# Row maxima of the attention scores, turned by VectorE in 32 by 32 blocks in place of TensorE

## The reference

```python
scores = jnp.einsum('bhqd,bhkd->bhqk', Q, K) / scale
scores = jnp.where(mask, scores, NEG_INF)
attention = jax.nn.softmax(scores, axis=-1)
heads_out = jnp.einsum('bhqk,bhkd->bhqd', attention, V)
```

## Time and profile before

| | |
|---|---|
| runs | 1285.56, 1286.76 (median) and 1288.77 us |
| span of the profiled execution | 1284.1 us, 2.7 us under the median of the runs |
| busy in it | PE 94%, DVE 70%, ACT 55%, POOL 37% of the span |
| TensorE's granted clock, mean | 0.987 |
| transfers `QS<-NT` | 64, of 12 KB each |

### The profile page before, as it was taken

One profiled execution on the slowest core, in us unless ns is written; L12 is line 12 of the kernel. 1 busy time (PEld: TensorE's weight loads), 2 busy tenths in 40 slices (PEclk: granted clock), 3 DMA queues, 4 the chain that ended last, 5 costly groups with the idle time before them and its releaser, 6 DMA issues.

```text
span 1284.1 us, 25175 instructions
## 1 busy us (share of the span) xinstructions
PE 1213.3 (94%) x9260; PEld 859.1 (67%) x9260; DVE 893.2 (70%) x2680; ACT 710.7 (55%) x1197; POOL 481.3 (37%) x675
## 2 busy tenths in 40 slices
PE   7899999999999989999999989999999999988998
PEld 6577666666767654444458866677676776578987
DVE  4677677876787646589999856767867868652333
ACT  2455555555655538889973426666566566622221
POOL 5534333443443100067000334344643643322555
PEclk9899999999999999999999999999999999998999
DMA  6423333233432041000004653355455342137973
GB/s 194 127 77 105 91 93 108 88 105 98 123 88 67 11 128 55 1 1 2 1 1 130 177 157 108 108 152 147 129 167 136 113 134 72 51 145 241 311 194 39
DMA packets 121942, 137.22 MB, mean 107 GB/s; under 512 B 12882, under 2 KB 116428, under 8 KB 121798
## 3 DMA queue, kind: packets, MB, share of 16 engines
q1 hardware_dynamic: 111888, 125.98, 33.2%
q0 software_dynamic: 7296, 8.15, 3.5%
q10 hardware_dynamic: 2634, 1.49, 0.5%
HBM read 58.42 MB, written 27.36 MB: 67 GB/s over the span
## 4 chain that ended last, share of the span: by engine, by line
PE 55%; DVE 6%; issue 3%; ACT 2%; POOL 1%; SPq 1%; DMA 1%; ACTq 0%; POOLq 0%; DVEq 0%
PE PS L669 14%; PE PS L715 6%; PE PS L470 5%; PE PS L410 5%; PE PS L683 4%; PE PS L453 4%; PE PS L429 4%; PE PS L528 2%; PE PS L724 2%; PE PS L502 2%; PE PS L417 2%; DVE NM L1119 1%; PE PS L546 1%; ACT P L839 1%; PE PS L511 1%
## 5 line engine op out<-in xcount | busy, mean ns | idle before, releaser
L839 ACT ACTIVATE P<-PS 128x512 f32<-128x512 f32 x512 | 302.4, 601 | 165.8 <-PE PS L456 100.2
L1116 DVE CUSTOM_DVE_ANT_0 MX<-PS,NQ 128x256 bf16<-128x256 f32 x512 | 192.5, 418 | 73.3 <-PE PS L429 73.0
L453 PE MATMUL PS<-QS,KS 99*128 99x256 bf16 x1024 | 226.6, 275 | 7.7 <-ACT P L839 6.7
L1119 DVE TENSOR_REDUCE NM<-PS 128x2 f32<-128x512 f32 x256 | 173.5, 685 | 74.6 <-PE PS L429 72.9
L429 PE MATMUL PS<-KS,QS 96*128 96x256 bf16 x1024 | 196.9, 275 | 21.6 <-DVE NM L1116 13.4
L429 PEld LDWEIGHTS PS<-KS,QS 96*128 96x128 bf16 x1024 | 87.2, 98 | 86.6 <-DVE NM L1116 26.1
L470 PE MATMUL PS<-P,V 128*32 128x256 f32 x2048 | 137.7, 387 | 1.5 <-ACT P L839 1.5
L453 PEld LDWEIGHTS PS<-QS,KS 99*128 99x128 bf16 x1024 | 95.4, 99 | 53.3 <-ACT P L839 20.1
L456 PE MATMUL PS<-NK,identb 128*128 128x256 bf16 x512 | 128.2, 275 | 0.0
L669 PE MATMUL PS<-XNT,wup 128*128 128x512 f16 x576 | 124.9, 379 | 0.0
L669 PEld LDWEIGHTS PS<-XNT,wup 128*128 128x128 f16 x576 | 56.2, 98 | 67.3
(11 more groups left out here) (233 smaller groups left out, 2473.6 us busy)
## 6 DMA issues: line engine op xcount, KB each, us to landing
KS<-PP SPq DMA_DIRECT2D x192, 128.0 KB, 2.9
QS<-PP SPq DMA_DIRECT2D x192, 128.0 KB, 2.5
WH<-in_wex SPq DMA_DIRECT2D x16, 768.0 KB, 8.0
WG<-in_wex SPq DMA_DIRECT2D x10, 768.0 KB, 5.1
bufd<-bias_row SPq DMA_DIRECT2D x5, 1032.0 KB, 12.0
XB<-in_x SPq DMA_DIRECT2D x16, 256.0 KB, 2.8
CT<-in_ctxT SPq DMA_DIRECT2D x16, 256.0 KB, 3.1
x1d<-XB SPq DMA_DIRECT2D x16, 256.0 KB, 2.1
```

Source lines behind the costliest of these rows:

```text
L453: ins = tensor.matmul(o, t.KS[b % 3][0:99, h, 128 * kt:128 * kt + 128], t.QS[b % 3][0:99, h, :], start=True, stop=(L == 1))
L839: scalar.activation(t.P[h % 8][:, :, :], PS[:, h % 2, :].rearrange("p (k n) -> p k n", k=2), ACT.Exp).then_inc(s_ex, 1)
L1116: ins = vector.tensor_tensor_reduce(t.MX[:, 2 * (h % 2) + qt, :], PS[:, bk, 256 * qt:256 * qt + 256], t.NQ[b % 4][:, qt, :], -1.0, 1.0e30, ...
L1119: ins = vector.tensor_reduce(nm[:, :, h], PS[:, bk, :].rearrange("p (t n) -> p t n", t=2), X, ALU.max, negate=True)
```

## The change

TensorE no longer turns the maxima, and ACT no longer copies them. The parts stand in `NP` as 32 columns for each of the two query tiles (24 used, 8 zeroed once for each layer by `pool_pad`). A new function `dve_maxima` transposes `NP`, 128 by 64, into `NT` with one DVE instruction, which turns each 32 by 32 block by itself. `NT` then has in its partition block `i` (32 partitions, 24 of them used) the queries 32i to 32i+31 of both tiles. So `act_maxima` issues four transfers in place of one, a block each, and each piece that lies together in memory on the `QS` side is 32 numbers, 64 bytes, in place of 256 numbers, 512 bytes. `pe_scores_t` waits for 64 counts in place of 16. Everything else stands as it was.

```diff
-            t.NT = [tile(m, f"NT{i}", [24, 256], BF16) for i in range(2)]
+            t.NT = [tile(m, f"NT{i}", [128, 64], BF16) for i in range(2)]
...
-            t.NP = tile(m, "NP", [128, 2, 3, 8], BF16)
+            t.NP = tile(m, "NP", [128, 2, 32], BF16)
...
-        def pe_maxima(L, b, hh):
-            n, t = L * NB + b, TL[L]
-            bk = odd_bank(("nt", n, hh), s_nt, 2 * n + hh + 1)
-            pe.wait_ge(s_np, 2 * n + hh + 1)
-            for qt in range(2):
-                ins = tensor.transpose(PSH[0:24, bk, 128 * qt:128 * qt + 128],
-                                       t.NP[:, qt, :, :].rearrange("p a h -> p (a h)"), identb[:, :])
-            ins.then_inc(s_ntr, 1)
...
-            pe.wait_ge(d_n[h // 8][b % 3], 16 * uses(L, b, 3))
+            pe.wait_ge(d_n[h // 8][b % 3], 64 * uses(L, b, 3))
...
-            for b, hh in maxima_at(L, s, k, 10, 2):
-                pe_maxima(L, b, hh)
...
         def act_maxima(L, b, hh):
             n, t = L * NB + b, TL[L]
-            bk = home["nt", n, hh]
-            if b:
-                act.wait_ge(d_n[hh][(b - 1) % 3], 16 * uses(L, b - 1, 3))
-            act.wait_ge(s_ntr, 2 * n + hh + 1)
-            scalar.activation(t.NT[hh][:, :], PSH[0:24, bk, 0:256], ACT.Copy).then_inc(s_nt, 1)
-
             act.wait_ge(s_nt, 2 * n + hh + 1)
             act.wait_ge(s_st, 16 * (n - 2))
-            scalar.dma_start(t.QS[b % 3][96:99, 8 * hh:8 * hh + 8, :], t.NT[hh][:, :]).then_inc(d_n[hh][b % 3], 16)
+            dst = t.QS[b % 3][96:99, 8 * hh:8 * hh + 8, :].rearrange("a h (t i r) -> a h t i r", t=2, i=4)
+            for i in range(4):
+                scalar.dma_start(dst[:, :, :, i, :], t.NT[hh][32 * i:32 * i + 24, :].rearrange("p (t r) -> p t r", t=2)).then_inc(
+                    d_n[hh][b % 3], 16)
...
+        def dve_maxima(L, b, hh):
+
+            n, t = L * NB + b, TL[L]
+            if b:
+                dve.wait_ge(d_n[hh][(b - 1) % 3], 64 * uses(L, b - 1, 3))
+            dve.wait_ge(s_pad, L + 1)
+            dve.wait_ge(s_np, 2 * n + hh + 1)
+            vector.transpose(t.NT[hh][:, :], t.NP[:, :, :].rearrange("p t c -> p (t c)")).then_inc(s_nt, 1)
...
             for h in scores_at(L, s, k):
                 dve_max(L, s + 1, h)
+            for b, hh in maxima_at(L, s, k, 10, 2):
+                dve_maxima(L, b, hh)
```

More of the change, by code:

```diff
@@ L339, in build @@
         d_n = [[sem(f"d_n{i}{j}") for j in range(3)] for i in range(2)]
-        d_i, s_iv = sem("d_i"), sem("s_iv")
+        d_i, s_iv, s_pad = sem("d_i"), sem("s_iv"), sem("s_pad")
         s_av, s_pen, s_var, s_rs, s_xn, s_xb = (sem(n) for n in ("s_av", "s_pen", "s_var", "s_rs", "s_xn", "s_xb"))
@@ L343, in build @@
         s_hi, s_r1, s_mid, s_lo = (sem(n) for n in ("s_hi", "s_r1", "s_mid", "s_lo"))
-        s_s, s_mx, s_np, s_ntr, s_nt = (sem(n) for n in ("s_s", "s_mx", "s_np", "s_ntr", "s_nt"))
+        s_s, s_mx, s_np, s_nt = (sem(n) for n in ("s_s", "s_mx", "s_np", "s_nt"))
         s_st, s_ex, s_ah, s_ot = (sem(n) for n in ("s_st", "s_ex", "s_ah", "s_ot"))
@@ L1649, in pool_maxima, with pool_pad @@
             v = t.NM[b % 2][:, :, 8 * hh:8 * hh + 8]
+            parts = [t.NP[:, :, 8 * a:8 * a + 8] for a in range(3)]
             pool.wait_ge(s_mx, 16 * n + 8 * hh + 8)
-            pool.wait_ge(s_ntr, i)
-            gpsimd.tensor_copy(t.NP[:, :, 0, :], v).then_inc(*pool.tick())
+            pool.wait_ge(s_nt, i)
+            gpsimd.tensor_copy(parts[0], v).then_inc(*pool.tick())
             pool.wait_ge(*pool.last())
-            gpsimd.tensor_tensor(t.NR[:, :, :], v, t.NP[:, :, 0, :], ALU.subtract).then_inc(*pool.tick())
+            gpsimd.tensor_tensor(t.NR[:, :, :], v, parts[0], ALU.subtract).then_inc(*pool.tick())
             pool.wait_ge(*pool.last())
-            gpsimd.tensor_copy(t.NP[:, :, 1, :], t.NR[:, :, :]).then_inc(*pool.tick())
+            gpsimd.tensor_copy(parts[1], t.NR[:, :, :]).then_inc(*pool.tick())
             pool.wait_ge(*pool.last())
-            gpsimd.tensor_tensor(t.NP[:, :, 2, :], t.NR[:, :, :], t.NP[:, :, 1, :], ALU.subtract).then_inc(s_np, 1)
+            gpsimd.tensor_tensor(parts[2], t.NR[:, :, :], parts[1], ALU.subtract).then_inc(s_np, 1)
+        def pool_pad(L):
+            gpsimd.memset(TL[L].NP[:, :, 24:32], 0.0).then_inc(s_pad, 1)
         def pool_scatter(g, i):
@@ L1726, in pool_program @@
             pool_setup()
+            pool_pad(0)
             for i in range(3):
@@ L1747, in pool_program @@
             pool_low(1, 1, 1)
+            pool.wait_ge(s_gu, NCH)
+            pool_pad(1)
             pool_maxima(1, 0, 0)
```

## The result

The changed kernel takes 1477.7 us (median of four runs, 1476.0 to 1480.0) against 1286.9: 1.1485 times as long, with a 95% interval of 1.1467 to 1.1503. The forecast was 1434 us with a range of 1370 to 1515. So the direction and the range hold, and the size is 44 us short. The profiled execution has a span of 1478.7 us, 194.6 more than before.

What follows compares the result with a forecast made beforehand. PE, busy 94% of the span, was taken as the bound. Late exponentials of 119 us, less 6 of waits, plus 34 of clock made 147 on a span of 1284.1; with 2.7 between span and median, 1434 us, range 1370 to 1515.

Steps and rivals of the forecast that it cites:

- The issue holds ACT: On ACT at slots 10 and 2: no exponential starts during an issue, so four in a row block four times that long.
- Price of an issue: On ACT: each of the four issues takes 0.77 us with its gap, 3.08 us for four.
- The bound of 1.21: Upper bound in us for an ACT issue if time grows with pieces; as a rival, 1575 us in all, 13% chance.
- Transposition: On DVE behind the slot's maximum: 0.23 us for 128 by 64 in bf16, plus 0.05 us to hand over.
- Late exponentials: At slots 10 and 2 of both layers, PE's scores start late by 1.17 to 2.85 us a place, 119 us in all.
- The 13 us of its transposes: PE's two transposes, 0.21 us each of 64 times, 13.4 us, go but lie inside the wait and shorten nothing.
- What comes off: PE's waits for maxima behind the stall shrink while DVE catches up: 6 us less.
- What the clock adds: After the 30 long waits at slot 10, 3.4 us of work each loses a third to half clock: 34 us.
- The landings: The four transfers land late but not too late, so PE does not wait for them at heads 0 or 8: no cost.
- issues of about 0.95 us: Upper end of the range: dearer issues on ACT with some clock loss at slot 2, giving 1515 us.
- likeliest case: The stall with 0.73 to 0.85 us an issue and clock lost at some or all slot 10 waits: 1400 to 1480, 65%.

Runs made afterwards that it cites:

- 3: Changed kernel with SP issuing the same four transfers in the same slots, nothing of the maxima left on ACT: 1275.4 us, 0.9920 of the kernel before.
- 4: Changed kernel with the four issues still on ACT, but one in each of four slots in a row: 1300.1 us, 1.0123 of the kernel before.
- experiment 5: Changed kernel with VectorE's transposition ahead of the slot's maximum, the four issues still on ACT: 1405.3 us, 1.0941 of the kernel before.
- 2: Kernel before, keeping TensorE's transposes and ACT's copy, its one transfer cut into four of 64 columns issued in a row from ACT: 1379.6 us, 1.0745.

## Why the prediction was right, and where its size was off

- **The issue holds ACT.** Right, shown by 3 and 4: taken off ACT the four issues cost nothing, taken apart 13 us of the 191. What holds PE is not how much ACT does but how long it starts nothing.
- **Price of an issue.** 0.77 from one to the next, forecast from one transfer's 0.73 and SP's gap; measured 3.05 for four, 0.77 each. The bound of 1.21 by the number of pieces was far off: 48 pieces cost 9 ns more than 24. (For the pieces' size the forecast had a sixth of SP's; 64 bytes to 1 KB is a sixteenth. Nothing in the sum hangs on it.) The Trainium skill calls the time to initiate a transfer "usually small relative to the DMA itself" ("DMA: Bandwidth & Descriptors", Issuing engines are not separate DMA queues). Here it is 0.74 us, and on ACT it isn't small for the kernel. The same section says that issuing from several engines only saves the sequencer's time of issuing, and that saving is just what 3 shows.
- **Transposition.** 0.23 forecast, 0.236 measured; 0.05 to hand over, 0.03 measured. At the place shown, 0.19 us lie between the end of the maximum (399.38) and the first issue, for 0.28 forecast.
- **Late exponentials: 119 us.** PE waits 140.0 - 6.7 = 133 us more. The 13 us of its transposes lie inside these waits, as forecast, so PE is late by 120. At the place shown head 13's product comes 3.94 us after head 10's maximum has ended (399.38 to 403.32), before it came 1.16 us after it (277.00 to 278.16): late by 2.78, against 2.85. But that 119 and 120 meet is luck in part. The forecast counted every place as a wait for an exponential, and 10.7 us more of waiting for ACT are in other rows (18.4 for 7.7): at three places of slot 2 PE waits for ACT's copy into `PP` in place of the exponential, and longer, and at the start of layer 0, which the forecast had left out, it waits 3.5 us for the copy into `XT`. With them PE is late by 131.
- **What comes off, 6 us.** PE's waits for maxima are 16.8 us in all for 19.7 before (9.4 and 7.4 for 13.4 and 6.3), so 3; another 3 (2.9) are waits of the transposes for their parts, which went with them and weren't in the sum.
- **What the clock adds: 34 us. This is the term that was mis-sized; by the runs it is about 73.** I had charged 30 stretches of 3.4 us with a third each. There were 207 - 33 = 174 us at half clock in place of 102: some waits come with twice as long a stretch, and some of those at slot 2 of layer 1 (1.6 us) have one too, while those of 1.3 us at slot 2 of layer 0 have none, nor have two at slot 10 (2.8 us at 199.89, 2.6 at 944.00). And the price was 0.42 in place of a third, since the row that I took for half clock (1.62 us) had run partly at the whole; in full half clock the same products take 1.94. 174 x 0.42 = 73 us. PE's busy time says the same: 57 us more with the 13 of the transposes gone, so 71 us more for the same work. With it the sum is 131 - 6 + 73 = 198, against 194.6 between the two spans.
- **The same account for two runs that had no part in the 0.42.** In experiment 5, 53 us less of waits for ACT, 2 more for maxima and 70 x 0.42 = 29 of clock are 80; between the spans it is 77. In 2, 71.5 us more of waits, 3 less for maxima and 44 x 0.42 = 18 of clock are 87 for 94. So the split is good to some 7 us, and what makes up the rest wasn't looked for.
- **The landings** of the maxima never held PE in the changed kernel. In 3 they did for 11 us, when SP was late.
- **The range.** It reached 1515 for issues of about 0.95 us with some clock lost at slot 2. Of these only the second came. The measured 1477.7 lies at the upper end of what the forecast calls its likeliest case, 1400 to 1480.

## What to carry to other kernels

An instruction stream that another engine waits for every microsecond or two should not issue several transfers in a row: each of those here was 0.73 to 0.74 us in which it started nothing else, for 3 KB as for 12 KB (other shapes took 0.29 to 0.60). Give them to SP, or spread them one to each wait; before that, look how far the waiting engine may run ahead. When a wait of TensorE grows past what it had before, charge the clock that may come with it as well: here it was nearly four tenths of the loss.

## What the runs showed of the hardware

- An issue's time on the queue hardly depends on how many pieces a transfer into three partitions has: 0.729 us for 24 pieces of 512 bytes, 0.728 for 24 of 128 bytes (experiment 2), 0.738 for 48 of 64 bytes.
- The half clock fell on the work behind the wait: wholly at the place shown (1.00 from 399.60 to 403.50, 0.51 from 403.50 to 406.90), and but for its first 1.5 us where the stretch was twice as long and began in the wait (0.50 from 1031.60 on, with work from 1033.16 on). 2.40 us of idle products in a wait of 2.98 were enough to cut the time at half clock by more than half, 86 us for 207, for a gain of 50 us.
- An issue of ACT ran beside the instruction ahead of it (280.75 for 280.73 in experiment 4) and held the one behind it.
- VectorE turns 128 by 64 in bf16 in 0.236 us, with 0.03 us to ACT's issue.
